# Experts' rows added to X by the indirect DMA itself instead of by GpSimd, with the fetch two tiles ahead

## What is computed

```
x = x + tanh(g_xattn[0]) * attention(layernorm(x), ctx)          # 16 heads
x = x + tanh(g_ffn[0])  * (shared(layernorm(x)) + routed(...))    # one expert of 8 for each token
x = x + tanh(g_xattn[1]) * (rmsnorm(layernorm(x)) @ W_in.T + b + depooled context patches)
x = x + tanh(g_ffn[1])  * sum over the two chosen experts of (h * x) @ expert_w
```

## Time and profile before

| | |
|---|---|
| median of the runs | 490.39 us (489.52 to 491.38) |
| profiled execution, span from first to last instruction | 490.0 us |
| mean granted TensorE clock | 0.972 |
| busy, share of the span | PE 91%, DVE 75%, POOL 65%, ACT 57% |
| busy of POOL's gathers L641 | 32 of them, 32.5 us |
| busy of POOL's additions L659 | 32 of them, 467 ns in the median |

### The profile page before, as it was taken

One profiled execution on the slowest core, in us unless ns is written; L12 is line 12 of the kernel. 1 busy time (PEld: TensorE's weight loads), 2 busy tenths in 40 slices (PEclk: granted clock), 3 DMA queues, 4 the chain that ended last, 5 costly groups with the idle time before them and its releaser, 6 DMA issues. The chain is left out here.

```text
span 490.0 us, 20510 instructions
## 1 busy us (share of the span) xinstructions
PE 443.7 (91%) x6871; PEld 349.2 (71%) x6872; DVE 366.8 (75%) x1201; ACT 277.8 (57%) x775; POOL 319.4 (65%) x780
## 2 busy tenths in 40 slices
PE   5789999989999999997987999987997799899998
PEld 3456677756766666774666988864655799898997
DVE  3668999978898989944768666545766678788984
ACT  2468899877988888764234545434233434444431
POOL 3845765567777777767723666577825899898630
PEclk9889999998999999989999999998999699999999
DMA  7941231111111110100245776631000011111001
GB/s 232 413 152 41 48 36 27 26 31 40 28 32 33 30 36 22 37 20 18 76 131 158 228 227 216 222 121 37 18 5 13 16 46 33 46 37 37 23 23 33
DMA packets 37394, 37.38 MB, mean 76 GB/s; under 512 B 20440, under 2 KB 31504, under 8 KB 36816
## 3 DMA queue, kind: packets, MB, share of 16 engines
q0 software_dynamic: 7552, 20.20, 12.9%
q1 hardware_dynamic: 29200, 16.06, 11.9%
q10 hardware_dynamic: 576, 0.26, 0.2%
HBM read 24.82 MB, written 7.86 MB: 67 GB/s over the span
## 5 line engine op out<-in xcount | busy, mean ns | idle before, releaser
L979 DVE TENSOR_REDUCE negm<-PS 128x4 f16<-128x512 f32 x128 | 81.9, 681 | 0.4
L716 ACT ACTIVATE pexp<-PS 128x512 f32<-128x512 f32 x128 | 69.4, 595 | 6.4 <-PE PS L1383 5.8
L1725 PE MATMUL PS<-w,vp 128*128 128x128 f32 x512 | 63.3, 277 | 0.0
L1725 PEld LDWEIGHTS PS<-w,vp 128*128 128x128 f32 x512 | 60.6, 194 | 0.0
L1396 PEld LDWEIGHTS PS<-pexp,vp 128*32 128x32 f32 x2048 | 34.5, 113 | 26.4 <-issue 20.5
L1396 PE MATMUL PS<-pexp,vp 128*32 128x64 f32 x2048 | 50.3, 230 | 0.3
L1619 PE MATMUL PS<-xsT,wst 128*128 128x128 f32 x320 | 44.4, 282 | 3.0 <-DVE stack L1217 1.3
L1619 PEld LDWEIGHTS PS<-xsT,wst 128*128 128x128 f32 x320 | 38.8, 191 | 7.3 <-issue 5.0
L581 POOL DMA_INDIRECT sorted_x<-VALL,posu x32 | 33.3, 1040 | 13.4 <-issue 7.6
L611 POOL DMA_DIRECT2D wst<-in_rt_gate_up_dram x40 | 21.5, 538 | 29.2 <-PE PS L1619 19.9
L1310 DVE TENSOR_TENSOR vp<-PS,xnT 128x1024 f32<-128x1024 f32 x32 | 38.6, 1205 | 0.8 <-PE PS L1702 0.8
(11 more groups left out here) (246 smaller groups left out, 1254.5 us busy)
## 6 DMA issues: line engine op xcount, KB each, us to landing
wst<-in_rt_gate_up_dram POOLq DMA_DIRECT2D x40, 256.0 KB, 3.5
xs<-sorted_x SPq DMA_DIRECT2D x40, 64.0 KB, 2.8
sorted_y<-YS POOLq DMA_DIRECT2D x40, 64.0 KB, 3.0
out_dram<-X SPq DMA_DIRECT2D x32, 64.0 KB
X<-in_x_dram SPq DMA_DIRECT2D x1, 1536.0 KB, 8.2
CK<-in_ctx_k_dram SPq DMA_DIRECT2D x1, 1536.0 KB, 12.2
CV<-in_ctx_v_swapped_dram SPq DMA_DIRECT2D x1, 1536.0 KB, 16.6
rdn<-in_rt_down_dram POOLq DMA_DIRECT2D x1, 1024.0 KB, 10.6
```

The source lines that it names most:

```text
L716: nc.scalar.activation(pexp[:, j, :], PS[:, 2 + j % 2, :], ACT.Exp).then_inc(S["exped"], 1)
L979: dve.tensor_reduce(negm[:, a.par, :, j], PS[:, j % 2, :].rearrange("p (g k) -> p g k", g=G), AX.X, ALU.max, negate=True).then_inc(S["maxe ...
L1725: nc.tensor.matmul(PS[:, 6 + y.par, 0:D], z[:, y.par, e, :], w1[:, e * D:e * D + D], start=(e == 0), stop=False)
```

## The change

The indirect DMA writes to X itself with an addition (`compute_op=ALU.add`); GpSimd's addition L659 and the semaphore `l_x2` go, and VectorE's statistics L1279 wait for the DMA's semaphore. As the DMA now changes X, it waits for `h_added` of its four tiles. The fetch starts two tiles ahead instead of three, and from tile 2 on it waits for the statistics of the tile that is two behind (`l_stats`), the one that used the same semaphore `y_in` before.

```
-    AHEAD = 3
+    AHEAD = 2
...
             def gather(t):
-                pool.indirect_dma_start(out=XN2[:, t, 0:D], out_offset=None, in_=sorted_y,
-                                        in_offset=bass.IndirectOffsetOnAxis(ap=places[:, t:t + 1], axis=0))\
+                if t % CT == 0:
+                    pool.wait_ge(S["h_added"], Tile(t // CT).done())
+                pool.indirect_dma_start(out=X[:, t * D:t * D + D], out_offset=None, in_=sorted_y,
+                                        in_offset=bass.IndirectOffsetOnAxis(ap=places[:, t:t + 1], axis=0),
+                                        compute_op=ALU.add)\
                     .then_inc(y_in[t % 4], 16)
...
             def last_step(stage):
                 x, v, f, a = (stage(i) for i in (0, 2, 4, 6))
-                if x:
-                    if x.t + AHEAD < NT:
-                        gather(x.t + AHEAD)
-                    if x.slot == 0:
-                        pool.wait_ge(S["h_added"], Tile(x.quad).done())
-                    pool.wait_ge(y_in[x.slot], 16 * (x.quad + 1))
-                    pool.tensor_tensor(X[:, x.cols(D)], X[:, x.cols(D)], XN2[:, x.t, 0:D], ALU.add)\
-                        .then_inc(S["l_x2"], 1)
+                if x and x.t + AHEAD < NT:
+                    if x.t >= 2:
+                        pool.wait_ge(S["l_stats"], Tile(x.t - 2).done())
+                    gather(x.t + AHEAD)
...
                 if w:
-                    dve.wait_ge(S["l_x2"], w.done())
+                    dve.wait_ge(y_in[w.slot], 16 * (w.quad + 1))
                     dve.bn_stats(st[:, w.par, :], X[:, w.cols(D)]).then_inc(S["l_stats"], 1)
```

More of the change, by code:

```diff
@@ L389, in flamingo_gated_two_layers @@
             S["c_" + n] = sem("c_" + n)
-        for n in ("x2 stats moments vars roots means shifts hn_ready hnT_done hnT_kept added mixed x3 stats2 moments2 "
+        for n in ("stats moments vars roots means shifts hn_ready hnT_done hnT_kept added mixed x3 stats2 moments2 "
                   "normed xnT_done xnT_kept routed choice spread mask_turned mask_kept masked "
@@ L491, in _ @@
             quad_credit(pool, ("k_score", 2), ("k_summed", 3))
-            credit(pool, *((n, 1) for n in "l_x2 l_vars l_roots l_means l_shifts l_added".split()))
+            credit(pool, *((n, 1) for n in "l_vars l_roots l_means l_shifts l_added".split()))
             pool.memset(idle[:], 0.0).then_inc(idle_zero, 1)
```

## The result

The changed kernel takes 493.94 us in the median of nine runs (489.87 to 496.93), beside 491.58 (489.52 to 498.39) for the kernel before on the same chips: ratio 1.0067, interval 1.0036 to 1.0098, so by the ratio it is 3.3 us slower (1.8 to 4.8). Timed once more in six runs it came to 493.80 against 489.62, ratio 1.0083 (1.0022 to 1.0144). The forecast was 486.2, in a range of 483.2 to 497.0: the range holds, the sign does not.

A forecast was written before the change was run, and what follows sets the result against it. The last stage was taken as bound by GpSimd at 3.43 us a tile, TensorE next at 3.03. Change 21 d - 8.4 us, with d = 0.2: 490.4 - 4.2 = 486.2 us; range 483.2 to 497.

The forecast's parts named there:

- the third: Part 3, GpSimd's adding gather: writing it costs d more than the plain gather's 1.026 us, taken as 0.2 us.
- d: GpSimd's extra time to write an adding gather over the plain 1.026 us; taken as 0.2 us, counted 21 times.
- a second lookup: Upper case for d at GpSimd's gather: the add looks rows up again, d = 0.48, total 492.1 us.
- a second pass: Upper case for d at GpSimd's gather: the whole gather's work again, d = 1.03, total 503.6 us.
- Rival (b): Gather in steps 9 to 29: add makes GpSimd write a second full pass, slower from d = 0.40; chance 0.20.
- The 0.42 us a step for the addition: Part 1, GpSimd steps 9 to 28: removing addition L659 saves 20 x 0.42 = 8.4 us.
- The semaphore's change: Part 2, VectorE's statistics L1279 wait for the DMA instead of GpSimd: landing hides within 8.2 us, cost nothing.
- rival (c): VectorE's L1279: landing later than 8.2 us makes everything wait; at 9 us +12, some 500 us; chance 0.04.
- The gather's wait for the statistics: Part 4, GpSimd's queue: always met from step 7; in steps 2 to 5 `vv` 0.8 us later plus d, hidden.
- The last gather in step 29: Part 5, moved from step 28: step 29 takes 3.01 + d instead of 2.37 us; TensorE's 3.03 covers all but d.
- Rival (d): GpSimd's removed addition was hidden anyway, nothing changes, 490.4 us; d from 0.3 to 0.48, the same in effect, chance 0.12.
- The cap: Part 6, last stage: TensorE's own 3.03 us step limits the gain to 6.7 us at d = 0.

## Why the prediction was wrong, point by point

The bound was read rightly. GpSimd paced the stage from step 9 to the last gather, and TensorE was next: with the add's price gone, 5.4 us came off, with GpSimd's addition on VectorE 6.5.

The step that failed is the third, the size of d. It was taken as 0.2 us, by scaling: half of a direct transfer's 0.542 for a third side of each row, less a share of fixed cost. The gather took 1.62 us, so d is 0.59. Scaling by rows was the mistake: from 64 to 128 rows the add's price grows by 0.06 us only, and nearly all of it is the fixed share that was taken off. Its own prices, a second lookup at 0.48 and a second pass at 1.03, lie on either side of d; I gave d over 0.48 a chance of a fifth, since both stood for work per row. With d = 0.59 the sum is 21 x 0.59 - 8.4 = +4.0 us, beside 3.3 by the ratio and 4.57 in the stretch, of which the unforeseen step of 4.36 is 0.8. That it also gives 494.4 us, beside the 493.94 measured, is in part luck: the kernel before had 490.39 then and 491.58 beside the changed one. Rival (b) was right in its direction, in its place and in the d at which the sum turns (0.40), but not in its mechanism: a second full pass would have been 1.03 us and half as much for half the rows, and a second lookup would have cost nothing in the direct DMA, which pays 0.29.

The 0.42 us a step for the addition is right: with 0.57 us of filler GpSimd's step was 3.58, which is 3.01 + 0.57. The semaphore's change hid: L1278 did not wait for a DMA. The landing was 3.4 us, under the 8.2 allowed; rival (c) is out. The gather's wait for the statistics was met from step 7 on, and cost nothing before. In step 5 `roots` came 29.38 us after the last copy of the sorted stage (355.56 - 326.18), 27.73 before (355.92 - 328.19): 1.65 us later, where 0.8 plus d, 1.4 with the measured d, was forecast, and it hid. The last gather in step 29 cost nothing that can be seen where it was moved alone. Rival (d), nothing changes, is out by the two intervals.

The cap was a little off: 6.7 us forecast at d = 0, 5.4 measured with the forecast's own edit, as the step there is 3.07; 6.5 in the version with 3.01. One step of 4.37 in the adding kernels was not foreseen.

What the prediction took from the Trainium skill ("DMA: Bandwidth & Descriptors", sections "SWDGE vs HWDGE vs iDMA" and "SDMA does more than copy"), a pair of descriptors for each operation and the add as a reduction of two streams, pointed the right way: d is above zero, 0.59. The prediction's own step from there, one more to write for each row, is not what an estimated 0.49 us of fixed price look like.

Of what would show it: GpSimd's step was to be 3.01 + d, and is 3.60; L1287's wait was to shrink to 0.45 and grew to 0.82; L1701's was to fall under 0.1 and is 0.44 in a common step. All three follow d. The start of the whole stage was to match to 0.3 us and came 2.0 us earlier (326.18 against 328.19), but from there to GpSimd's gather of step 9 it is 52.58 us against 52.52. TensorE's step with GpSimd out of its way was 3.01 or 3.07, and the half clock did not last longer.

## What to carry to other kernels

An operation that is folded into a DMA isn't gone: ask what its issuing engine pays to write the DMA, and when no trace has that price, don't only scale it by rows: cost the case in which it is fixed for each instruction too, as it nearly was here. Where the issuing engine is itself the bound, the fold must cost it less than the operation did, here 0.59 against 0.42 us. The cheaper way was to give the operation to the engine that waits for the bound one: 0.20 us on VectorE for 0.42 on GpSimd.

## What the runs showed of the hardware

What GpSimd pays for a gather hardly hangs on its rows: 0.97 us for 64, 1.02 for 128. A direct DMA of 128 rows took it 0.54 us as a store and 0.60 in the gather's place. The add puts 0.54 to 0.60 us on a gather and 0.29 on a direct DMA. The instruction behind an adding gather is recorded from 1.06 us after its start, as behind a plain one (1.05 to 1.09), and then lasts 0.6 us longer: the added time shows in two places of the timeline, and summing busy times would count it twice. The transfer's side of the add was cheap: 0.8 us more to landing, and a larger DMA share (0.24 for 0.13), of which nobody felt anything.

The larger share comes with packets, not with bytes. GpSimd's queue between 405 and 450 us, before and then after (packets, MB, share of 16 engines):

```profile
q0 software_dynamic: 416, 0.85, 7.5%
...
q0 software_dynamic: 1728, 0.79, 14.6%
```

That is 32 packets a gather before (13 gathers) and 144 with the add (12 gathers). Over the whole kernel an adding gather has 112 packets more with 128 rows (11136 in this queue against 7552, over 32 gathers) and 48 more with 64 rows (9088 against 7552), the direct add also 112. So with the add each row moves as a packet of its own, where the plain gather has 16 larger ones. GpSimd's price doesn't follow this count: 0.60 us at 112 packets more and 0.54 at 48.
